# LoRA-B gathered ahead of the second half of x, LoRA-A fetched by SyncE alone, the t chain ahead of the LoRA-B splits

## What is computed

```python
# 1. gated FFN, hidden width 1376, with a rank-16 adapter chosen for each batch
gate = x @ W_gate.T + 0.5 * (x @ A_gate[itok[b]].T) @ B_gate[itok[b]].T
up   = x @ W_up.T   + 0.5 * (x @ A_up[itok[b]].T)   @ B_up[itok[b]].T
act  = silu(gate) * up
d    = act @ W_down.T + 0.5 * (act @ A_down[itok[b]].T) @ B_down[itok[b]].T
# 2. linear layer with 8 summed LoRAs, residual
x2 = x + d @ W.T + bias + lora(d)
# 3. conditional linear layer, then a mixture of 64 rank-16 experts, top 16 of each token
c   = x2 @ W1.T + b1 + coeff[b] * (x2 @ (2 * mask[b] - 1))
out = x2 + 2 * sum_k gate_k * (c @ A_k.T) @ B_k.T
```

## Time and profile before

| | us |
|---|---|
| median of 3 runs | 363.18 (362.2 to 363.3) |
| profiled execution, its time | 365.2 |
| profiled execution, its span | 363.5 |
| TensorE (PE) busy | 356.8 (98%) |
| VectorE (DVE) busy | 198.0 (54%) |
| ACT busy | 141.6 (39%) |
| GpSimd (POOL) busy | 89.5 (25%) |

### The profile page before, as it was taken

One profiled execution on the slowest core, in us unless ns is written; L12 is line 12 of the kernel. 1 busy time (PEld: TensorE's weight loads), 2 busy tenths in 40 slices (PEclk: granted clock), 3 DMA queues, 4 the chain that ended last, 5 costly groups with the idle time before them and its releaser, 6 DMA issues.

```text
span 363.5 us, 4759 instructions
## 1 busy us (share of the span) xinstructions
PE 356.8 (98%) x1728; PEld 301.0 (83%) x1728; DVE 198.0 (54%) x302; ACT 141.6 (39%) x192; POOL 89.5 (25%) x95
## 2 busy tenths in 40 slices
PE   8997999999999999999999999999999999999997
PEld 7786888888888888998888898888888888888886
DVE  1838645554355434466565567579978877511101
ACT  3637641434144323345474354539343353201100
POOL 3757778545430000300000000000023065002200
PEclk9998999999999999999999999999999999999999
DMA  7934453321320014639524406401033012201011
GB/s 255 288 138 145 110 160 105 98 87 58 115 96 19 0 28 147 202 126 386 183 60 169 134 2 257 206 0 58 2 111 122 2 58 58 60 29 58 31 58 58
DMA packets 14914, 38.86 MB, mean 107 GB/s; under 512 B 2368, under 2 KB 4160, under 8 KB 13616
## 3 DMA queue, kind: packets, MB, share of 16 engines
q1 hardware_dynamic: 11584, 30.75, 24.8%
q0 software_dynamic: 2880, 7.48, 7.0%
q10 hardware_dynamic: 432, 0.39, 0.3%
HBM read 36.51 MB, written 2.10 MB: 106 GB/s over the span
## 4 chain that ended last, share of the span: by engine, by line
PE 91%; DMA 3%; POOL 2%; ACT 1%; issue 1%; DVE 1%; POOLq 0%; SPq 0%
PE ps L1030 28%; PE ps L1031 28%; PE ps L1032 27%; PE ps L1050 3%; PE ps L1152 3%; DMA b_raw<-b_gu,row_of 2%; POOL b_raw L376 1%; PE ps L1242 1%; DMA small_sb<-small_in 1%; PE ps L1229 1%; ACT t_st L432 1%; ACT b_st L432 1%; DVE b_st L699 1%; PE ps L1251 0%; POOLq L364 0%
## 5 line engine op out<-in xcount | busy, mean ns | idle before, releaser
L1030 PE MATMUL ps<-x_hl,w_hl 128*128 128x512 f32 x160 | 63.2, 395 | 0.0
L1031 PE MATMUL ps<-x_hl,w_hl 128*128 128x512 f32 x160 | 63.2, 395 | 0.0
L1032 PE MATMUL ps<-x_hl,w_hl 128*128 128x512 f32 x160 | 62.6, 391 | 0.0
L376 POOL DMA_INDIRECT b_raw<-b_gu,row_of x44 | 45.1, 1026 | 35.0 <-DVE b_st L699 22.8
L415 POOL TENSOR_TENSOR am_hl<-am_raw,am_hl 128x512 fp32r<-128x512 f32 x8 | 11.2, 1405 | 136.7 <-ACT am_hl L432 136.7
L720 DVE TENSOR_TENSOR glu<-glu,ps 128x512 f32<-128x512 f32 x22 | 15.0, 684 | 39.4 <-PE ps L1050 39.4
L1032 PEld LDWEIGHTS ps<-x_hl,w_hl 128*128 128x128 f32 x160 | 30.3, 190 | 6.7
L432 ACT ACTIVATE act<-glu 128x512 f32 (+1 forms) x22 | 13.8, 631 | 55.0 <-DVE glu L720 51.7
L1030 PEld LDWEIGHTS ps<-x_hl,w_hl 128*128 128x128 f32 x160 | 30.4, 190 | 5.4
L1031 PEld LDWEIGHTS ps<-x_hl,w_hl 128*128 128x128 f32 x160 | 30.5, 191 | 4.9
L1030 PE MATMUL ps<-act,wd_hl 128*128 128x512 f32 x80 | 31.1, 389 | 0.0
(11 more groups left out here) (136 smaller groups left out, 700.3 us busy)
## 6 DMA issues: line engine op xcount, KB each, us to landing
wc_raw<-mask_w SPq DMA_DIRECT2D x8, 1024.0 KB, 7.2
w_raw<-w_gu SPq DMA_DIRECT2D x9, 512.0 KB
wd_raw<-w_dn SPq DMA_DIRECT2D x10, 256.0 KB
x_raw<-x_t SPq DMA_DIRECT2D x8, 256.0 KB, 6.7
w_raw<-w_t SPq DMA_DIRECT2D x2, 1024.0 KB, 7.3
x<-x_t SPq DMA_DIRECT2D x2, 1024.0 KB, 6.3
am_raw<-a_moe SPq DMA_DIRECT2D x8, 256.0 KB, 2.6
bm_raw<-b_moe SPq DMA_DIRECT2D x4, 512.0 KB, 3.8
```

Of the source, the lines that this page charges most:

```text
L376: nc.gpsimd.indirect_dma_start(b_raw[f % 2][:, p].rearrange("q m f -> q (m f)"), None, b_gu, bass.IndirectOffsetOnAxis(ap=row_of[:, f, p:p ...
L1030: nc.tensor.matmul(out, w_high, m_high, start=start, stop=False)
L1031: nc.tensor.matmul(out, w_high, m_low, start=False, stop=False)
L1032: return nc.tensor.matmul(out, w_low, m_high, start=False, stop=stop)
```

## The change

`small_in` is issued by GpSimd as its first DMA instead of SyncE. SyncE loads LoRA-A of all eight batches, and x half 1 behind them. GpSimd makes the row numbers, waits for the first slice of x, issues w for k=2,3, and then gathers LoRA-B. A load of w for a later tile waits for the first gather of LoRA-B into the same slot. The high part of w for k=0 is made by VectorE. ACT and VectorE split x half 1 wholly behind LoRA-A, and both take t of half 0 ahead of LoRA-B 0.

```diff
--- before.py
+++ after.py
@@ -60,7 +60,6 @@
 NEG = -3.0e38
 WARM_UP = 10
 W_FIRST = 6
-A_BY_SP = 5
 AD_LOADS_AFTER = 3
 AD_SPLITS_AFTER = (5, 6, 7, 8)
 KB = 1024
@@ -190,7 +189,7 @@
         dma_x1 = [sem(f"dma_x1_{k}") for k in range(KD)]
         dma_w = [sem(f"dma_w{u}") for u in range(2)]
         dma_b = [sem(f"dma_b{u}") for u in range(2)]
-        dma_a, dma_a_pool, dma_ad = sem("dma_a"), sem("dma_a_pool"), sem("dma_ad")
+        dma_a, dma_ad = sem("dma_a"), sem("dma_ad")
         dma_wd = [sem(f"dma_wd{u}") for u in range(2)]
         dma_bd, dma_last, dma_lora, dma_ffn_w = sem("dma_bd"), sem("dma_last"), sem("dma_lora"), sem("dma_ffn_w")
         dma_x2 = [sem(f"dma_x2_{s}") for s in range(2)]
@@ -249,23 +248,23 @@
                 sp.dma_start(x_raw[:, k, 0:HALF], x_t[:, k, 0:HALF]).then_inc(dma_x0[k], 16)
 
             load_x0(0)
-            sp.dma_start(small_sb[:], small_in).then_inc(dma_small, 16)
             load_x0(1)
             for u in range(2):
                 sp.dma_start(w_raw[u][:, 1], w_gu[u, :, 1]).then_inc(dma_w_first[u][1], 16)
             for k in range(2, KD):
                 load_x0(k)
-            for k in range(KD):
-                sp.dma_start(x_raw[:, k, HALF:T], x_t[:, k, HALF:T]).then_inc(dma_x1[k], 16)
             sp.wait_ge(dma_small, 16)
-            for b in range(A_BY_SP):
+            for b in range(BATCH):
                 adapter = sp.value_load(itok_all[0:1, b:b + 1], min_val=0, max_val=ADAPTERS - 1)
                 sp.dma_start(a_raw[:, b].rearrange("q k m r -> q (k m r)"),
                              a_gu[bass.ds(adapter, 1)]).then_inc(dma_a, 16)
+            for k in range(KD):
+                sp.dma_start(x_raw[:, k, HALF:T], x_t[:, k, HALF:T]).then_inc(dma_x1[k], 16)
             sp.dma_start(const_sb[:], consts).then_inc(dma_const, 16)
 
             def load_tile(f, slot):
 
+                sp.wait_ge(dma_b[slot], 64)
                 for made in (w_hi, w_lo):
                     sp.wait_ge(made, W_FIRST + f - 3)
                 sp.dma_start(w_raw[slot][:], w_gu[bass.ds(f, 1)]).then_inc(dma_w[slot], 16)
@@ -356,19 +355,16 @@
 
         @block.gpsimd
         def _(pool):
-            for u in range(2):
-                pool.dma_start(w_raw[u][:, 2:KD], w_gu[u, :, 2:KD]).then_inc(dma_w_first[u][2], 16)
-
+            pool.dma_start(small_sb[:], small_in).then_inc(dma_small, 16)
             pool.wait_ge(dma_small, 16)
-            for b in range(A_BY_SP, BATCH):
-                adapter = pool.value_load(itok_all[0:1, b:b + 1], min_val=0, max_val=ADAPTERS - 1)
-                pool.dma_start(a_raw[:, b].rearrange("q k m r -> q (k m r)"),
-                               a_gu[bass.ds(adapter, 1)]).then_inc(dma_a_pool, 16)
             nc.gpsimd.tensor_scalar(itok_first[:], itok_own, RANK, None, ALU.mult).then_inc(row_step, 1)
             pool.wait_ge(row_step, 1)
             nc.gpsimd.tensor_tensor(row_of[:], row_sb, itok_first[:].unsqueeze(1).broadcast_to([P, FT, NPAIR]),
                                     ALU.add).then_inc(row_step, 1)
             pool.wait_ge(row_step, 2)
+            pool.wait_ge(dma_x0[0], 16)
+            for u in range(2):
+                pool.dma_start(w_raw[u][:, 2:KD], w_gu[u, :, 2:KD]).then_inc(dma_w_first[u][2], 16)
 
             def load_b(f):
 
@@ -476,22 +472,20 @@
                 act_e.wait_ge(dma_w_first[u][part], 16)
                 copy(w_hl[u][:, 0, ks], w_raw[u][:, ks]).then_inc(w_hi, 1)
 
-            for k in range(2):
-                x_high(k, 0)
-                for u in range(2):
-                    w_first_high(u, slice(k, k + 1), k)
+            x_high(0, 0)
+            x_high(1, 0)
+            act_e.wait_ge(w_hi, 2)
+            for u in range(2):
+                w_first_high(u, slice(1, 2), 1)
             x_high(2, 0)
             for u in range(2):
                 w_first_high(u, slice(2, KD), 2)
             x_high(3, 0)
-            for k in range(2):
-                x_high(k, 1)
-            act_e.wait_ge(dma_a, 16 * A_BY_SP)
-            act_e.wait_ge(dma_a_pool, 16 * (BATCH - A_BY_SP))
+            act_e.wait_ge(dma_a, 16 * BATCH)
             for m in range(2):
                 for par in range(2):
                     copy(a_part(a_st, m, 0, par), a_own(m, par)).then_inc(a_hi, 1)
-            for k in range(2, KD):
+            for k in range(KD):
                 x_high(k, 1)
 
             def t_high(g):
@@ -503,8 +497,8 @@
                 copy(t_st[64:96, two, 0], t_raw[0:32, two]).then_inc(t_hi, 1)
                 copy(t_st[0:32, two, 1], t_raw[64:96, two]).then_inc(t_hi, 1)
 
+            t_high(0)
             b_high(0, 0, 1)
-            t_high(0)
             b_high(1, 1, 1)
             w_high(2, 0, 2)
             for u in range(2):
@@ -735,6 +729,9 @@
                 dve.wait_ge(w_hi, n)
                 low(w_hl[u][:, 1, ks], w_raw[u][:, ks], w_hl[u][:, 0, ks]).then_inc(w_lo, 1)
 
+            for u in range(2):
+                dve.wait_ge(dma_w_first[u][0], 16)
+                nc.vector.tensor_copy(w_hl[u][:, 0, 0:1], w_raw[u][:, 0:1]).then_inc(w_hi, 1)
             for k in range(2):
                 x_low(k, 0)
                 for u in range(2):
@@ -743,15 +740,12 @@
             for u in range(2):
                 w_first_low(u, slice(2, KD), 5 + u)
             x_low(3, 0)
-            for k in range(2):
-                x_low(k, 1)
             for m in range(2):
                 for par in range(2):
                     dve.wait_ge(a_hi, 2 * m + par + 1)
                     low(a_part(a_st, m, 1, par), a_own(m, par), a_part(a_st, m, 0, par)).then_inc(a_lo, 1)
-            for k in range(2, KD):
+            for k in range(KD):
                 x_low(k, 1)
-            b_low(0, 0)
             dve.wait_ge(dma_const, 16)
 
             def t_mask(g):
@@ -767,6 +761,7 @@
 
             t_mask(0)
             t_low(0)
+            b_low(0, 0)
             b_low(1, 1)
             w_low(2, 0)
             t_mask(1)
```

## The result

The changed kernel is slower. Its median is 364.44 us against 362.42 us, a ratio of 1.0048 with a 95% interval of 1.0027 to 1.0069; on another chip it was 1.0049 (1.0036 to 1.0062). That is 1.7 to 1.8 us by the ratios and 2.0 by the medians, where 3.0 us of gain were forecast and the range ended at 362.4. (The 363.18 that the prediction starts from is the median of the first three executions of the kernel before; 362.42 is that of ten.)

The account below looks back on a forecast made before the run. TensorE was taken as the bound, so only its idle time or a higher clock could pay. Starting project(1,1) 1.9 us sooner plus 1.1 us at full clock gave 3.0 us, from 363.18 to 360.2, range 358.8 to 362.4.

Parts of the forecast that it names:

- (g): Sum: project(1,1) starts at 29.2 instead of 31.13, 1.9 us, plus 1.1 us at full clock; 3.0 us gained.
- (d): Half 1 of x behind LoRA-A on SyncE: 3.6 us landing, last piece at 19.8, its low part done at 21.15.
- (a): First pass: 0.63 us wait at k=1 gone, 0.2 us gained at its start; TensorE at lora_down at 16.96.
- (f): GpSimd's gathers: LoRA-B 0 there at 18.8, wanted 24.5; w (k=2,3) issued 6.25 to 7.55, with up to 4 us to land.
- (b): small_in from GpSimd: issued at 1.40, 3.63 us to land, there at 5.03; bounds 3.3 to 7.7.
- (c): LoRA-A by SyncE alone: eight loads, 1.14 us a step; lora_down starts at 18.6 after a new 1.64 us stall.
- Rival 4: Half 1 of x or small_in late, delaying t_mask(0); 1.5 us slower, 364.7, deciding from about 5.2 us landing; chance 0.09.
- (e): The t chain: t_mask(0) starts at 21.15 instead of 24.19, earlier spacings kept, LoRA-B 1 releases TensorE at 28.5.
- rival 3: A new wait at tile 2's LoRA-B, at worst 2.0 us of stall; gain 1.0, 362.2; chance 0.06.
- rival 2: w (k=2,3) late by the 6.3 us landing, TensorE stalls 2.3 us at k=2; gain 2.3, 360.9; chance 0.08.
- Rival 1: The clock falls anyway, after the new stall before lora_down, 1.6 us lost; gain 1.4, 361.8; chance 0.18.

Follow-up runs that it names:

- experiment 1: The kernel before, unchanged, profiled again, with its executions listed by mean granted clock; ratio 1.0015 to itself.
- before_again: The kernel before, no edit, profiled a second time; ratio 1.0015 (1.0001 to 1.0029), profiled execution 363.8 us.
- after_again: The changed kernel, unchanged, run again beside its variants on one chip; ratio to the kernel before 1.0049, profiled execution 367.15 us.
- experiment 8: Two edits of the changed kernel: LoRA-A shared again by SyncE (five) and GpSimd (three), 0.9994; SyncE's added wait for LoRA-B removed, 1.0112 (to the kernel before).
- a_no_b_wait: The changed kernel without SyncE's wait for LoRA-B ahead of a later tile's w; ratio to the kernel before 1.0112.
- T first: The kernel before with only t of half 0 put ahead of LoRA-B 0 on ACT and VectorE; 361.2 us, ratio 0.9973.
- experiment 5: The kernel before with t ahead of LoRA-B 0 and all eight LoRA-A loads on SyncE, half 1 of x still ahead; ratios 1.0098 and 1.0136.
- a_small_sp: The changed kernel with small_in issued by SyncE again, half 1 of x still behind LoRA-A; ratio to the kernel before 1.0027.
- a_x1_ahead: The changed kernel with half 1 of x issued ahead of LoRA-A on SyncE again; 362.24 us, ratio to the kernel before 0.9997.

## Why the prediction was wrong

Two steps failed: the base of the sum in (g), which counted 2.8 us as gain that most executions couldn't give, and the landing of half 1 of x in (d), which put t 2.5 us late.

**The base of the sum.** This is the first step that failed: "The median of the runs is 363.18, 2.0 below; the same gain gives 360.2." The 2.0 us between the profiled execution and the median were the thing to explain. The profiled one had the low clock (1.5 us) and LoRA-B 0 landing 1.3 us later than in the second profile; by the list of executions and the sums in experiment 1 most have neither, though none without the fall was profiled. A gain worked out from its rows counted 1.07 us of clock in `project(1,1)` and a start of it at 31.13. Without both causes that start is 29.39 (before_again's 29.82, less the 0.43 that its four matmuls lost to the clock). So 1.07 + (31.13 - 29.39) = 2.8 of the 3.0 us were not there to be won. Against 29.39, the changed kernel's 31.61 is 2.2 us late, where the medians say 2.0. The forecast of 360.2 is 4.2 us under the measured 364.4: 2.8 by the base and 2.2 by the late chain, less 0.8 because the median of ten executions of the kernel before is that much under the median of three.

**(a) first pass.** It was to end 0.83 us sooner, at 16.96, and ended at about 18.0 (19.03 less the wait of 0.99). Right is that the wait at k=1 goes, but the second profile of the kernel before doesn't have it either. The two copies on VectorE took 0.29 us each, within the bounds; what was missed is that the second waits for its w to land with x's low part queued behind it, a wait of 0.3 us for TensorE (1.4 in after_again). Another 0.4 us went at k=2, see (f).

**(b) `small_in`.** Mis-sized: 4.78 us instead of 3.63 (4.4 to 5.5 in all kernels with it on GpSimd, 3.4 to 4.0 on SyncE). The Trainium skill, DMA: Bandwidth & Descriptors, section "Latency and other measured facts", gives about 1 us to the first byte from GpSimd and about 0.6 from SyncE, 0.4 apart. The profiles show the whole landing and not the first byte; it is about 1.1 us longer from GpSimd, so the 0.4 was too little for it.

**(c) LoRA-A.** The step held, 7.15 to 14.97 being 1.12 us each, and so did the start of `lora_down` (19.03 for 18.6). The stall ahead of it was 0.99 us instead of 1.64, because TensorE came a good 1 us later than forecast. What was missed is the weight of the eight loads: they were counted as a stall on TensorE's own path. Sharing them again gives 2.0 us back, and the chain in experiment 8 shows it come by x and t behind them.

**(d) half 1 of x.** The second step that failed, and the term that turned the sign: 5.56 us to the landing of the last piece instead of 3.6. With the issue 0.55 us late (16.75 for 16.2, which is what was left of the late `small_in`), this makes the 2.5 us by which the mask is late. The reason given, that neither the first w nor the loads of tiles 2 and 3 run beside it, left out what does: the gathers of LoRA-B 1 and `consts`, and from 20.05 the loads of tiles 2 and 3 after all. The window of the changed kernel has the DMA engines full (share 1.02):

```profile
18.00:22.00 4.00, 3.01 (x22) 2.83 (x22) 2.20 (x6) 2.22 (x5) 1.40 (x2) 1.00 1.02 335
```

That this lengthens the landing fits a_no_b_wait, where the loads left 2.3 us sooner and the landing took 6.02 us; no run takes away the gathers or `consts` alone. `consts` itself was late in the same way, by the DMA issues of the changed kernel (us to landing last):

```profile
const_sb<-consts SPq DMA_DIRECT2D x1, 232.0 KB, 5.9
```

Issued at 17.23, it landed at 23.1 instead of 20.45, only 0.5 us before `t_mask(0)` started. So half 1 of x could have been at most 0.5 us faster before `consts` held the mask in its place.

Rival 4 named this place and the point from which it decides, 5.2 us, and gave it 0.09 with `small_in`; both of its causes came, each by part. Its time, 364.7, is near the measured 364.4 by luck: it was 1.5 us above 363.18, with the clock falling and `project(1,1)` starting at 32.6, where the start was 31.61 at full clock in the profile and the loss 2.0 us above 362.42.

**(e) the t chain.** Its spacings held: 23.61 to 31.06 is 7.45 us, 21.15 to 28.5 was 7.35. It was late as a whole by 2.5 us.

**(f), (g).** The gathers had cover as said, and no wait came at tile 2 (rival 3). w (k=2,3) had not: it left at 7.65 instead of 6.25, since it stands behind the late `small_in` on GpSimd, and was split from 11.58 on. TensorE, due at 12.04, started k=2 at 12.26 and lost 0.4 us by the end of the pass; the later wait for LoRA-A hid it. That is rival 2, in small. Rival 1, the clock after the new stall, did not show in either profile. In 4 of the changed kernel's 17 executions the mean clock was 0.995 or less; the one of them that was profiled (after_again) has no stall ahead of `lora_down`, and its clock falls at k=0 and at `adapt_first(0)`. Nothing was lost behind `project(1,1)`.

How the loss divides, by undoing one part at a time: LoRA-A shared 2.0 us, x ahead of it 1.8 and, not clear of noise, `small_in` by SyncE 0.5 to 0.8, while T first brings 1.0 in the kernel before and SyncE's wait 2.3. By the traces the first two are one loss seen from two sides, a chain from LoRA-A over x to t, and shouldn't add; no run undoes both.

## What to carry to other kernels

Before summing a gain from a profile, set its own time against the median of the runs; if it is 0.8% above, find what in it the median doesn't have (here a fall of the clock and a late landing of LoRA-B 0), and count nothing of that as gain. A queue that issues loads one after the other with an index read each works in series, here 1.1 us a step, and all that is issued behind it, down to the mask of another chain, moves with it. Where a change has five parts, the one with the clear gain (here the order of two splits) is worth timing alone.

## What the runs showed of the hardware

- The granted clock fell to 0.50 after waits of TensorE of 0.5 and 1.7 us, or after 1.7 alone, and the mean clock was 0.995 or less in 17 of 110 executions of one kernel, at a cost of 1.5 us. With the eight loads behind half 1 of x (experiment 5, waits of 3.2 and 4.9 us in the two profiles) all 13 executions had 0.995 or less.
- Waits of the same size went either way: after 1.44 and 0.78 us the clock fell (after_again), after 1.43 and 0.78 it didn't (a_small_sp); after 1.73 alone it fell (before_again), after 1.77 alone it didn't (a_x1_ahead).
- SyncE's register instructions took 0.65 to 0.71 us instead of 0.15 to 0.29 in two profiled executions of 368.1 us, between 11.6 and 18 us; in two others with the same order of loads they mostly kept their usual length. The cause is open.
- A 256 KB load landed after 2.6 us on a quiet queue and after 5.56 us here; a 32 KB load took 3.4 to 4.0 us by SyncE and 4.4 to 5.5 us by GpSimd at the start of the kernel. The last gather of LoRA-B 0 landed after 6.3 us in one profile of the kernel before and after 4.7 in the other.
- Two timings of one kernel gave intervals that don't meet (0.9911 to 0.9959, 0.9971 to 1.0009), and the kernel before against itself gave 1.0001 to 1.0029: half a per cent is near what one such comparison can carry.
